# Rolling the middle 26 steps of a fully unrolled cross-attention and RWKV kernel into a loop over pairs of steps

## The reference, cut to what matters

```python
# layer 0: cross attention, channels = 128, tokens = 512
Mn = Wn @ inorm(x_c) + bn ;  Mm = Wm @ inorm(x_s) + bm
A  = softmax(Mn^T Mm) ;      x = Wo @ ((Wl @ x_s + bl) @ A^T) + bo + x_c
# layer 1: RWKV block on 128 tokens of width 512, 32 heads of 16
xa = ln(x); sx = shifted(xa) - xa
xk, xw, xv, xr, xg = xa + sx * (maa_stack + tanh((xa + sx*maa_x) @ maa_w1) @ maa_w2)
w = exp(-exp(time_decay + tanh(xw @ td_w1) @ td_w2)); r, k, v, g = projections
for each token t:  out = r_t (u*a + s);  s = a + w_t * s      # a = outer(k_t, v_t), 16x16 per head
x1 = x + (groupnorm(out) * g) @ Wo.T
return x1 + sigmoid(xr2 @ Wfr.T) * (relu(xk2 @ Wfk.T)**2 @ Wfv.T)
```

## Time and profile before

| | |
|---|---|
| median of 3 runs | 2310.23 us (2308.37 to 2310.74) |
| the profiled execution | 2308.37 us |
| its span, first to last instruction | 2306.2 us |
| mean granted clock of the tensor engine | 0.953 of full speed |
| vector engine busy | 1993.5 us, 86% |
| tensor engine busy (matmul) | 1971.5 us, 85% |
| GpSimd busy | 1118.4 us, 48% |
| ScalarE busy | 904.6 us, 39% |

### The profile page before, as it was taken

One profiled execution on the slowest core, in us unless ns is written; L12 is line 12 of the kernel. 1 busy time (PEld: TensorE's weight loads), 2 busy tenths in 40 slices (PEclk: granted clock), 3 DMA queues, 4 the chain that ended last, 5 costly groups with the idle time before them and its releaser, 6 DMA issues. The chain is left out here.

```text
span 2306.2 us, 34734 instructions
## 1 busy us (share of the span) xinstructions
PE 1971.5 (85%) x12548; PEld 1364.5 (59%) x12548; DVE 1993.5 (86%) x2788; ACT 904.6 (39%) x1793; POOL 1118.4 (48%) x818
## 2 busy tenths in 40 slices
PE   6778898889898889899889889888889888999746
PEld 3556665556666556666555666555666555666624
DVE  3698899988999898899898989998898998899872
ACT  3334434344433443434444443434443334444111
POOL 1344555454555554455545455545455555445431
PEclk8999999999999999999999999999999999999877
DMA  5232232222232232232222223222223222222220
GB/s 199 76 86 83 79 88 78 82 78 81 83 91 79 80 83 79 78 89 78 82 81 79 85 82 88 79 81 77 83 82 87 80 81 83 76 76 81 78 60 9
DMA packets 86136, 189.17 MB, mean 82 GB/s; under 512 B 18800, under 2 KB 35312, under 8 KB 84944
## 3 DMA queue, kind: packets, MB, share of 16 engines
q1 hardware_dynamic: 64464, 170.19, 25.8%
q10 hardware_dynamic: 21504, 16.78, 2.4%
HBM read 161.78 MB, written 16.78 MB: 77 GB/s over the span
## 5 line engine op out<-in xcount | busy, mean ns | idle before, releaser
L605 DVE TENSOR_TENSOR_SCAN S<-wrep,S 128x1024 f32<-128x1024 f32 x256 | 605.8, 2366 | 3.4
L430 POOL TENSOR_TENSOR xf<-xf,xa 128x512 f32<-128x512 f32 x160 | 321.9, 2012 | 285.5 <-DVE xf L570 281.1
L446 POOL COPY S<-s 128x8 f32<-128x8 f32 x256 | 283.5, 1108 | 310.2 <-PE bank L1071 276.7
L614 DVE TENSOR_TENSOR S<-S,rT 128x1024 f32<-128x1024 f32 x256 | 363.3, 1419 | 3.4
L596 DVE TENSOR_TENSOR S<-vrep,kT 128x1016 f32<-128x1016 f32 x256 | 341.5, 1334 | 0.0
L400 POOL TENSOR_SCALAR rstd<-mv 128x1 f32<-128x1 f32 (+1 forms) x96 | 102.3, 1066 | 489.5 <-DVE mv L534 302.1
L1071 PE MATMUL bank<-S,slide 128*32 128x256 f32 x2048 | 176.1, 418 | 130.5 <-DVE S L614 130.5
L570 DVE SCALAR_TENSOR_TENSOR xf<-bank,par,sx 128x128 f32<-128x128 f32 x640 | 179.1, 341 | 59.2 <-PE bank L1031 56.4
L957 PE MATMUL bank<-xf,Wk 128*128 128x128 f32 x1024 | 128.4, 286 | 66.9 <-ACT prob L778 63.6
L402 POOL TENSOR_TENSOR hrs<-hrs,mhalf 128x32 f32<-128x32 f32 x32 | 175.5, 5486 | 2.7
L1071 PEld LDWEIGHTS bank<-S,slide 128*32 128x32 f32 x2048 | 41.5, 111 | 224.0 <-DVE S L614 161.7
(11 more groups left out here) (124 smaller groups left out, 3607.1 us busy)
## 6 DMA issues: line engine op xcount, KB each, us to landing
vrep<-v_dram SPq DMA_DIRECT2D x256, 512.0 KB
xc<-x_c SPq DMA_DIRECT2D x32, 256.0 KB, 2.6
xs<-x_s SPq DMA_DIRECT2D x32, 256.0 KB, 3.0
xres<-xin SPq DMA_DIRECT2D x32, 256.0 KB, 2.4
v_dram<-vT ACTq DMA_DIRECT2D x32, 256.0 KB, 2.3
out<-rr ACTq DMA_DIRECT2D x32, 256.0 KB, 2.9
Wv<-big_w SPq DMA_DIRECT2D x1, 1024.0 KB, 8.2
Wk<-big_w SPq DMA_DIRECT2D x1, 1024.0 KB, 10.0
```

Source lines behind the costliest of these rows:

```text
L430: po.tensor_tensor(xf[:, b, :, :], xf[:, b, :, :], xa[:, :, 1:P + 1], ALU.add).then_inc(pool_mid.sem, 1)
L446: po.tensor_copy(S[:, u % 2, :, 0], s0[:, p, k:k + UJ]).then_inc(pool_wkv.sem, 1)
L605: ve_.tensor_tensor_scan(s, wrep[:, u % C, :, :].rearrange("p j t -> p (j t)"), s, 0.0, ALU.mult, ALU.add).then_inc(dve_wkv.sem, 1)
L614: ve_.tensor_tensor(s, s, rT[:, p, u % C, :].unsqueeze(1).broadcast_to([P, UJ, P]), ALU.mult).then_inc(dve_wkv.sem, 1)
```

## The change

Steps 0 to 4 stay written out. Steps 5 to 30 become a loop of 13 passes on every engine, each pass two steps long so that the parity of every stage is known in the body. Steps 31 to 35 are written out again. The work, its order and the buffers are the same. In the loop body the element's number is an expression of the loop's index, so a count that a wait compares with, and the address of a load or store of element `n`, are worked out in registers at run time; `held` now does move values into registers there. `Fori` ends each pass with an addition to the index and a compare-and-branch back to the head of the body.

```diff
--- before.py
+++ after.py
@@ -32,6 +32,7 @@
 CONSTS = 10 + C
 LAG = {"att": 0, "mid": 1, "wkv": 2, "tail": 3, "fin": 4}
 STEPS = NB + 4
+FIRST = 5
 DM = 32
 DD = 64
 EPS = 1e-5
@@ -80,7 +81,13 @@
     def peeled(s):
         step(s, stages(s, lambda lag: ((s - lag) // 2, (s - lag) % 2)))
 
-    for s in range(STEPS):
+    for s in range(FIRST):
+        peeled(s)
+    pairs = (NB - FIRST) // 2
+    with eng.Fori(0, pairs) as i:
+        for k in (FIRST, FIRST + 1):
+            step(i * 2 + k, stages(i * 2 + k, lambda lag: (i + (k - lag) // 2, (k - lag) % 2)))
+    for s in range(FIRST + 2 * pairs, STEPS):
         peeled(s)
```

## The result

| | before, same chip | after |
|---|---|---|
| median | 2309.39 us (4 runs) | 2411.03 us (2405.19 to 2412.07, 4 runs) |
| ratio | | 1.0459, 95% interval 1.0428 to 1.0491 |
| profiled execution: time, span | 2308.37, 2306.2 us | 2429.17, 2426.9 us |
| mean granted clock of the tensor engine | 0.953 | 0.925 |

The loop makes the kernel slower by 101.6 us, 4.4%, by the medians of four executions each. The ratio is taken over more of them: the record has 21 executions of the kernel after, from 2402.90 to 2429.17 us with a median of 2416.86, which makes it 4.6%, some 106 us. The profiled execution is the longest of the 21. The forecast was 73 us slower. The page of the kernel after: its span, part 1 (busy us, share of the span, instructions), and from part 3 the two queues that carry instructions (packets, MB, share of 16 engines).

What follows compares the result with a forecast made beforehand. The prediction took a ring of short handoffs round a nearly full vector engine as the bound. The profiled 2308.4 us plus 37 for jumps and 36 for register work gave 2381 us, 8-in-10 range 2322 to 2470.

Steps and rivals of the forecast that it cites:

- the likeliest case: Whole kernel: jumps and register work both cost time, 2381 us, own range 2328 to 2445, given 55%.
- The sum: Whole kernel: profiled 2308.4 us plus 37 for jumps and 36 for registers makes 2381, 3.2% slower.
- The jump: Seam between passes: each jump back waits for an instruction packet, 3.1 us net, 12 times, 37 us.
- The register work: Counts for waits in steps 5 to 30: mostly hidden, 1.4 us exposed per step, 26 steps, 36 us.
- Upstream, again 0.7: Tensor engine, GpSimd and ScalarE: their register operations end the vector engine's waits later, 0.7 us per step.
- The gap at the seam: Vector engine between lines 586 and 596: a gap no semaphore explains, about 3 us; none or above 5 fails.
- Line 500 and 627 growing by 0.1 to 0.2 each: Vector engine's waits for GpSimd (line 500) and for C (line 627) grow by 0.1 to 0.2 us each.
- Packets of the second queue above one per pass and engine: Queue read as feeding all but the tensor engine: instruction packets stay above one per pass and engine.
- The body stays at hand: Rival, 15%: no jump waits for a packet, only 0 to 36 us of register work remain, 2310 to 2346.
- Fully exposed: Rival, 13%: all register work shows on the vector engine, 178 us on top of 37 for jumps, 2525 us.
- More than one packet per jump: Rival, 12%: each jump waits for two packets and a second engine, 96 us, with 36 for registers 2442.
- Faster: Rival, 5%: the body stays and instruction fetches stop competing with `vrep` loads, saving 6.6 us, about 2304.

Runs made afterwards that it cites:

- e1: Kernel after with steps 5 to 30 written out again, every count still worked out in registers, no jump: +94.2 us, 1.0410 of the kernel before.
- e2: Kernel after, loop kept, with a branch hint that asks for the body's head ahead of the jump back: 2398 us, 1.0404 of the kernel before.
- e5: Kernel after, on the vector engine alone all counts of an operation worked out ahead of its first wait: 2378 us, 1.0304 of the kernel before.
- e12: Kernel after with the vector engine alone written out with constants, the other four looping: +25.6 us, 1.0109 of the kernel before.
- e6: Kernel after with counts ahead of waits on vector, tensor, ScalarE and GpSimd engines, plus the branch hint: 2360 us, 1.0233 of the kernel before.
- e4: Kernel after with only the vector engine looping, the other four written out with constants: +121.5 us, 1.0525 of the kernel before.
- e9: Kernel before with seven unread matmuls in the tensor engine's idle time ahead of unit 0's sums: +3.6 us, 1.0014 of the kernel before.
- e11: e6 with seven unread matmuls in the tensor engine's idle time ahead of unit 0's sums: +58.2 us, 1.0245 of the kernel before.

## Why the prediction was right in direction and 29 us short

**Faster or slower, and the range: right.** 2411 us lies within 2322 to 2470 and within the likeliest case's own 2328 to 2445.

**The sum: in part luck.** Both of its terms lie at or outside the bounds that the prediction gave them. The jumps, forecast at 37 and between 13 and 54 us, came to 7 to 13; the registers, forecast at 36 and between 5 and 80, came to some 93. One was too high and the other too low, and so the sum stayed within the range.

**The jump: the stall right, its share on the path too high.** Forecast 3.15 us of stall on the vector engine; measured 3.21, 38.5 in all. But the step that took 3.1 of it as net, 37 us, failed: in the profiled execution it nets 1.8, and the timed runs of e1 and e2 leave 7 to 13 us for all twelve. The prediction had the wait for C end 3 us later too; instead C was there and the gap took the place of that wait. In e5, where that wait stays, a jump does net 3.0 us as forecast. Of the stalls forecast for the others the tensor engine's shows in 7 places (20.7 us, 2.96 each, in the wait list of the kernel after). Those of ScalarE and GpSimd, and with them the late `fin_kr` that was to hold up C, did not happen: their bodies are not fetched again, and at the seam shown `kk` starts 1.20 us after xhat (566.06 and 564.86 us), as in before (1031.57 and 1030.37). The Trainium skill's rule for a taken branch ("Runtime: NRT & Kernel Launch", "Instruction fetch mechanics") agrees with the trace in that the jump waits for a fetch. Its 512 instructions of room, by which the vector engine's body of 368 would fit, did not keep it at hand without the hint.

**The register work: the step that failed most.** The prediction put "10 x 0.07 = 0.7 us" on the vector engine and "again 0.7 us" upstream, 1.4 us a step and 36 us in all. e1 has no jump and is 94 us slower, 3.4 to 3.6 us a step. Point by point:

- The price of one: 0.07 us came from a wait that stands alone. Here one or two register operations follow the engine's own last result, 0.08 to 0.18 us at a place (e1 against before, by the starts of the operations within a step; the scan's idle time in after is 0.21). These delays sum to 1.4 us a step in e1: 0.27 at the first product (0.14 and 0.40 in turn, with the pair's own addition in every second step), 0.14 and 0.11 at unit 0's scan and last product, 0.18 at each of three later places and 0.08 to 0.11 at four. The forecast total was met, but on one engine.
- "Upstream, again 0.7": wrong place. The four other engines looping cost 25.6 us, their jumps included (e12), and the waits for GpSimd's roots were 68.8 us for 70.3.
- What was missing: the lost start, 2.5 us in 21 of 23 steps of e1, 2.3 a step, if it costs there what it costs in e6, and Kp at half clock, in 8 of 23 steps of e1 against 2. With 1.4 the lost start alone makes 3.7 for the 3.4 to 3.6 measured, so the terms overlap: in e5, where delays of some 0.1 us are left at five places, a step without jump or disturbance is only 0.3 us longer than before. That the two add up is arithmetic on readings and not an experiment of its own. The prediction did say that a small delay comes back several times round the ring, and gave it no term.
- "The vector engine's busy time unchanged at 1993 us": it rose to 2022.7. The lost start is in it only as an exchange, 28 us more on the last products, which the tensor engine waits for, and 27 less on `sx`, for which nothing waits long. Another 15 us are on the scans, perhaps by the same exchange, since GpSimd's column copies fell by 66 us; that was not followed up. The remaining 13 are mostly no longer work: operations that overlapped the one before them by some 0.1 us no longer do, so that the busy stretches join less (the durations themselves sum to only 18 us more).

**What would show it.** The gap at the seam: 3.21 us, right. Every second step longer by about 3 us: 1.8, wrong. Other steps at 69.5 us: 72.3, wrong. Line 500 and 627 growing by 0.1 to 0.2 each: neither grew; it was `nmax`, where the vector engine meets a tensor engine that unit 0 had delayed. Packets of the second queue above one per pass and engine: right in number, 5 per pass for four engines, but they are the vector engine's alone.

**The rivals.** *The body stays at hand*: refuted for the vector and the tensor engine (packets rose), true for the other three, and true for all with the hint, but at 2398 us and not at the 2310 to 2346 given, because of the registers. *Fully exposed*: refuted by e1, 94 us for 178. *More than one packet per jump*: the tensor engine's queue shows three packets within 5 us at a jump (418.7, 419.7, 423.8 us), but the vector engine's stall stays at 3.0 to 3.5 us, so it doesn't price the change. *Faster*: refuted.

**Open.** Why the loop on the vector engine alone costs more than on all. What puts Kp at half clock. Whether holding back `rku` would bring the loop close to the kernel before; this was not run. By the 11 steps of e6 that neither disturbance hit, 26 x (69.0 - 68.4) = 16 us would be left if the slow Kp went too; by all 16 steps with the start won, whose mean is 70.2 us against 68.5, it would be 26 x 1.7 = 44 of the 54. By this estimate `rku` alone would bring little.

## What to carry to other kernels

Counts in registers are paid where the engine has just waited for its own last result: work them out ahead of the wait (the same 12 additions cost 12 us and not 38), and give the branch back its hint. A delay of 0.1 us can go with 2.5 us a step when another engine's operation then wins the race against yours, so before pricing a small delay at its own length, look in the timeline for operations of two engines that start within it of each other and see which one is the slow one. Idle or half-clocked time removed from an engine is worth something only at the place on which the step waits; look for where it went before counting it.

## What the runs showed of the hardware that I had not expected

- Two operations of the vector engine and GpSimd that read at the same time: 1.24 and 2.25 us with 0.12 us of lead for the vector engine, in every step; with 0.01 us of lead either 1.23 and 2.35 or 2.36 and 1.27. The margin is a few nanoseconds wide: with 15 to 17 ns of lead the vector engine won 46 of 54 times, with 12 ns or less never.
- A loop body of 368 vector instructions is fetched again at each of 12 jumps, 3.21 us each; bodies of 236, 134 and 91 instructions on the three other engines of that queue are not. With the hint on the branch, packets of instructions fall from 115 + 80 to 26 + 19 and the gap to 0.56 us.
- The same gap of about 3.1 us cost 0, 1.8 and 3.0 us of the step (e4, after, e5).
- One or two register operations behind the wait for the engine's own last result cost 0.08 to 0.18 us (e1); 12 additions a step ahead of it cost 12 us in all, behind it 38.
- Filler matmuls before unit 0 raised the granted clock (e9: 0.953 to 0.973) and in e11 moved the half clock to Kp, which went from 144.4 to 182.2 us.
